# When and by which engine a 65 MB buffer is zeroed in a graph network kernel, and where its node features are loaded

## The reference, cut to what matters

```python
edge_index = jnp.stack([src, dst])
h = jnp.maximum(_layernorm(x, axis=-1), 0.0)
x = x + _L0_gnn_ref(h, src, dst, edge_weight, L0_gnn_kernel, L0_gnn_bias)
# in _L0_gnn_ref:
#   messages = edge_vals[:, None] * transformed[edge_col]
#   aggregated = segment_sum(messages, edge_row, num_segments=N_NODES)   # edge_row = src
```

## Time and profile before

| | us |
|---|---|
| median of 3 runs | 19079.15 (19072.6 to 19079.55) |
| span of the profiled execution | 19095.1 |
| `prepare` until VectorE's first cast | 195.2 |
| `prepare`, rest | 44 |
| `begin` | 60 |
| "gcn_in" | 104 |
| "hist", first block | 221 |

### The profile page before, as it was taken

One profiled execution on the slowest core, in us unless ns is written; L12 is line 12 of the kernel. 1 busy time (PEld: TensorE's weight loads), 2 busy tenths in 40 slices (PEclk: granted clock), 3 DMA queues, 4 the chain that ended last, 5 costly groups with the idle time before them and its releaser, 6 DMA issues. The chain is left out here.

```text
span 19095.1 us, 359029 instructions
## 1 busy us (share of the span) xinstructions
PE 12487.0 (65%) x80127; PEld 9630.4 (50%) x80128; DVE 13169.5 (69%) x30834; ACT 7233.3 (38%) x19056; POOL 11352.9 (59%) x11773
## 2 busy tenths in 40 slices
PE   3543337589998377775777757777587777753333
PEld 2322225456666266664666646666356666433332
DVE  4877778567776688887888878888555555543334
ACT  0111118345555266663666636666331111310000
POOL 0477760067776177773777737777027777047775
PEclk7555555577777555555655555555786666865555
DMA  5233334233334222222222222222672222841112
GB/s 192 62 94 93 94 83 115 61 90 102 103 103 92 52 58 58 58 58 46 58 58 58 58 46 58 58 58 58 240 270 53 53 53 51 337 156 26 26 26 47
DMA packets 1474194, 1652.50 MB, mean 87 GB/s; under 512 B 976447, under 2 KB 1080911, under 8 KB 1442001
## 3 DMA queue, kind: packets, MB, share of 16 engines
q1 hardware_dynamic: 1062709, 1057.28, 18.7%
q0 software_dynamic: 404480, 528.97, 14.0%
q10 hardware_dynamic: 6912, 65.18, 0.8%
HBM read 1028.20 MB, written 626.36 MB: 87 GB/s over the span
## 5 line engine op out<-in xcount | busy, mean ns | idle before, releaser
L1728 POOL DMA_INDIRECT gat_from_src<-gat_src_dram,gat_src_at x4992 | 4825.8, 967 | 2417.3 <-issue 1520.7
L2168 POOL DMA_INDIRECT rel_from_src<-typed_dram,rel_src_at x3328 | 3177.5, 955 | 2386.3 <-ACT rel_src_at L2182 1373.6
L1274 POOL DMA_INDIRECT all_node<-hyp_dst_dram,hyp_src_at x1768 | 1725.7, 976 | 1622.6 <-ACT hyp_src_at L1292 1084.7
L2298 PE MATMUL rel_ps_sum<-all_node,rel_msg 128*64 128x128 f32 x6656 | 1514.3, 403 | 1685.4 <-DVEq L2260 1656.2
L1945 PE MATMUL gat_ps_sum<-all_node,gat_msg 128*80 128x128 f32 x9984 | 2268.0, 420 | 42.1 <-DVE gat_msg L1841 7.5
L2298 PEld LDWEIGHTS rel_ps_sum<-all_node,rel_msg 128*64 128x64 f32 x6656 | 1211.3, 210 | 1936.6 <-DVEq L2260 1513.2
L1945 PEld LDWEIGHTS gat_ps_sum<-all_node,gat_msg 128*80 128x80 f32 x9984 | 2058.3, 251 | 102.3 <-issue 43.3
L776 POOL DMA_INDIRECT bucket_dram<-all_node,order_index x1664 | 1617.6, 972 | 530.8 <-issue 505.9
L1889 DVE TENSOR_TENSOR gat_sums<-gat_sums,gat_ps_sum 80x128 f32 x4992 | 1393.2, 279 | 381.3 <-DVE gat_sums L1889 212.5
L1851 DVE TENSOR_TENSOR_SCAN gat_ps_log<-gat_masks,gat_top,gat_ps_log 8x1024 f32<-8x1024 bf16 x624 | 1462.0, 2343 | 228.3 <-DVE gat_sums L1889 219.6
L1923 PE MATMUL gat_ps_log<-all_ident,gat_leaky 128*8 128x128 f32 x4992 | 1069.9, 387 | 727.0 <-DVE gat_leaky L1836 727.0
(11 more groups left out here) (445 smaller groups left out, 27294.7 us busy)
## 6 DMA issues: line engine op xcount, KB each, us to landing
typed_dram<-typed_res SPq DMA_DIRECT2D x200, 2144.0 KB
gat_relrow<-in_rows_dram SPq DMA_DIRECT2D x624, 256.0 KB
all_node<-gcn_table_dram SPq DMA_DIRECT2D x1664, 48.0 KB
gat_from_src<-gat_src_dram,gat_src_at POOLq DMA_INDIRECT x4992
bucket_dram<-by_dst_zero ACTq DMA_DIRECT2D x48, 1326.0 KB
gsum_rec<-bucket_dram SPq DMA_DIRECT2D x221, 288.0 KB
all_node<-lo_rows_dram SPq DMA_DIRECT2D x221, 256.0 KB
rel_table<-inv_count_dram SPq DMA_DIRECT2D x1664, 32.5 KB
```

Of the source, the lines that this page charges most:

```text
L1274: nc.gpsimd.indirect_dma_start(from_dst[:, q, k, :], None, g.hyp_dst[:, :], bass.IndirectOffsetOnAxis(ap=src_at[:, q, k:k + 1], axis=0)).t ...
L1728: nc.gpsimd.indirect_dma_start(from_src[:, q, k, :], None, g.gat_src[:, :], bass.IndirectOffsetOnAxis(ap=src_at[:, q, k:k + 1], axis=0)).t ...
L2168: nc.gpsimd.indirect_dma_start(from_src[:, q, k, :], None, g.typed[:, :], bass.IndirectOffsetOnAxis(ap=src_at[:, q, k:k + 1], axis=0)).the ...
L2298: last = nc.tensor.matmul(ps_sum[0:D, k, :], msg[:, q % 2, k, :], member[:, q, k, :], start=True, stop=True)
```

## The change

- The 48 clears move from ScalarE to POOL. A new function `clear_buckets` issues a part of them. It has two semaphores in turn, and before a clear it waits until the clear two before it has landed, so that at most two are under way.
- Clears 0 to 7 are issued at the end of POOL's stream of `prepare`, after waits for the seven edge tiles and for the node features. Clears 8 to 17 are issued in `begin`, clears 18 to 47 in the first block of "hist", after the iota.
- The node features are loaded in `prepare`, on SP right behind the seven edge tiles and ahead of SP's wait for the masks, into a buffer `g.x_all` that both phases share. VectorE sets its tail before it sets the tile of zeros. `begin` has no load and no wait for one.
- `rows` is no tile of its own any more but the same memory as `raw`, seen as floats: VectorE's casts run in place.
- In "order" POOL waits for two semaphores instead of one.

```diff
+def clear_buckets(nc, g, pool, first, last):
+    rows = g.bucket.rearrange("(p w) f -> p (w f)", p=P)
+    for n in range(first, last):
+        if n >= 2:
+            pool.wait_ge(g.zeroed[n % 2], 16 * (n // 2))
+        nc.gpsimd.dma_start(rows[:, n * ZERO:(n + 1) * ZERO], g.zero[:, :]).then_inc(g.zeroed[n % 2], 16)
...
 def prepare(nc, g):
-        rows = [ph.sb(f"rows{n}", [P, EB, P]) for n in range(5)]
+        rows = [raw[n][:, :, :].bitcast(F32) for n in range(5)]
...
                 nc.gpsimd.tensor_copy(g.iota16[:, :], g.iota[:, :])
+                pool.wait_ge(padded, 7)
+                pool.wait_ge(rows_in, 7 * 16)
+                pool.wait_ge(x_in, 32)
+                clear_buckets(nc, g, pool, 0, 8)
...
                                  ).then_inc(rows_in, 16)
+                sp.wait_ge(padded, 7)
+                full, rest = N // P, N % P
+                sp.dma_start(g.x_all[:, 0:full, :], g.x[0:full * P, :].rearrange("(t p) d -> p t d", p=P)).then_inc(x_in, 16)
+                sp.dma_start(g.x_all[0:rest, full, :], g.x[full * P:N, :]).then_inc(x_in, 16)
                 sp.wait_ge(stored, 1)
...
-            @block.scalar
-            def _(act):
-
-                act.wait_ge(padded, 6)
-                flat = g.bucket.rearrange("(p w) f -> p (w f)", p=P)
-                for n in range(CLEARS):
-                    act.dma_start(flat[:, n * ZERO:(n + 1) * ZERO], g.zero[:, :]).then_inc(g.zeroed, 16)
...
                 nc.vector.memset(padf[:, :], 0.0).then_inc(padded, 1)
+                nc.vector.memset(g.x_all[:, N // P:NT, :], 0.0).then_inc(padded, 1)
                 nc.vector.memset(g.zero[:, :], 0.0).then_inc(padded, 1)
...
 def begin(nc, g):
-        x, sq, stat = ph.sb("x", [P, NT, D]), ph.sb("sq", [P, NT, D]), ph.sb("stat", [P, 2, NT])
+        x, sq, stat = g.x_all, ph.sb("sq", [P, NT, D]), ph.sb("stat", [P, 2, NT])
         with nc.Block() as block:
+            @block.gpsimd
+            def _(pool):
+                clear_buckets(nc, g, pool, 8, 18)
+
             @block.sync
             def _(sp):
-                sp.wait_ge(cleared, 1)
-                sp.dma_start(x[:, 0:full, :], g.x[0:full * P, :].rearrange("(t p) d -> p t d", p=P)).then_inc(loaded, 16)
-                sp.dma_start(x[0:rest, full, :], g.x[full * P:N, :]).then_inc(loaded, 16)
-                sp.wait_ge(loaded, 32)
                 sp.dma_start(nodes_view(g.xs), x[:, :, :]).then_inc(stored, 16)
                 sp.wait_ge(stored, 16)
 
             @block.vector
             def _(dve):
-                nc.vector.memset(x[:, full:NT, :], 0.0).then_inc(cleared, 1)
-                dve.wait_ge(loaded, 32)
...
 def bucket_places(nc, g):
                                allow_small_or_imprecise_dtypes=True).then_inc(numbered, 1)
+                clear_buckets(nc, g, pool, 18, CLEARS)
...
 def edges_ordered(nc, g):
-                pool.wait_ge(g.zeroed, 16 * CLEARS)
+                for s in range(2):
+                    pool.wait_ge(g.zeroed[s], 16 * (CLEARS // 2))
```

More of the change, by code:

```diff
@@ L199, in floor_by @@
     chain(v.tensor_scalar(out, out, MAGIC, None, ALU.subtract))
+def clear_buckets(nc, g, pool, first, last):
[4 more added lines that the diff above has]
+        nc.gpsimd.dma_start(rows[:, n * ZERO:(n + 1) * ZERO], g.zero[:, :]).then_inc(g.zeroed[n % 2], 16)
 def prepare(nc, g):
     with Phase(nc, "prep") as ph:
-        loaded, padded, const, turned, copied, step, stored, rows_in = ph.sems(
-            "loaded padded const turned copied step stored rows_in")
+        loaded, padded, const, turned, copied, step, stored, rows_in, x_in = ph.sems(
+            "loaded padded const turned copied step stored rows_in x_in")
         padi = ph.sb("padi", [P, 16], I32)
@@ L404, in begin @@
     with Phase(nc, "begin") as ph:
-        loaded, step, cleared, stored, asked, given = ph.sems("loaded step cleared stored asked given")
-        x, sq, stat = ph.sb("x", [P, NT, D]), ph.sb("sq", [P, NT, D]), ph.sb("stat", [P, 2, NT])
-        full, rest = N // P, N % P
+        step, stored, asked, given = ph.sems("step stored asked given")
+        x, sq, stat = g.x_all, ph.sb("sq", [P, NT, D]), ph.sb("stat", [P, 2, NT])
         with nc.Block() as block:
+            @block.gpsimd
+            def _(pool):
+                clear_buckets(nc, g, pool, 8, 18)
             @block.sync
             def _(sp):
-                sp.wait_ge(cleared, 1)
-                sp.dma_start(x[:, 0:full, :], g.x[0:full * P, :].rearrange("(t p) d -> p t d", p=P)).then_inc(loaded, 16)
-                sp.dma_start(x[0:rest, full, :], g.x[full * P:N, :]).then_inc(loaded, 16)
-                sp.wait_ge(loaded, 32)
                 sp.dma_start(nodes_view(g.xs), x[:, :, :]).then_inc(stored, 16)
@@ L2401, in gnn_kernel @@
             g.base = own.sb("base", [1, ET], I32)
-            g.zero, g.zeroed = own.sb("zero", [P, ZERO]), own.sem("zeroed")
-            prepare(nc, g)
-            begin(nc, g)
+            g.zero, g.zeroed = own.sb("zero", [P, ZERO]), own.sems("zeroed0 zeroed1")
+            with Phase(nc, "whole") as whole:
+                g.x_all = whole.sb("x_all", [P, NT, D])
+                prepare(nc, g)
+                begin(nc, g)
             project(nc, g, "gcn_in", [w["L0_gnn_kernel"]], [(g.gcn_table, slice(0, D), slice(0, D))],
```

## The result

| | before | changed |
|---|---|---|
| median (range) of 4 runs, us | 19079.35 (19072.6 to 19079.69) | 18918.34 (18915.8 to 18919.41) |
| ratio, 95% interval | | 0.9916 (0.9902 to 0.993) |
| span of the profiled execution | 19095.1 | 18917.7 |
| VectorE's first cast in `prepare` | 195.2 | 47.6 |
| first reduction in `begin` (L386, now L397) | 258.4 | 100.3 |

The changed kernel is 161.0 us faster, where 148 were forecast. (The two profiled executions differ by more, 177.4 us: the one of the kernel before was 16 us slower than its median, and that difference lies in the later stages, see "The two kernels again".) VectorE's timeline of the changed kernel, beside the earlier trace rows, holds most of it. Columns are start, length, instruction, and in brackets the idle time before it with its releaser.

The account below looks back on a forecast made before the run. The first 195 us were taken as a DMA queue, with late-needed clears among urgent transfers. Terms -144 - 17.3 + 5 + 7 + 1 = -148.3 took the profiled span to 18946.8, hence 18931 us, range 18892 to 18980.

Parts of the forecast that it names:

- Part 1: Start of `prepare`: without clears ahead, edge loads land earlier and VectorE starts at 51 us, not 195.2: -144 us.
- Part 2: `begin`: features loaded early behind the edge loads land far ahead, so the wait for them goes: -17.3 us.
- Parts 3 and 4: Clears 0 to 7 in `prepare` +5 us, 8 to 17 in `begin` +7, first loads of "gcn_in" +1.
- SP waits for the stores, so the phase grows: End of `prepare`: SP's wait for mask stores, landing at 101 us against VectorE's 95.3, lengthens it by 5 us.
- the stores land when all of the clears are through: `prepare`: mask stores take turns with the clears and land last, at 101 us or one landing earlier.
- How engines share: DMA engines: one short row of a load moves for each row of the clears, 0.42 us a row.
- Part 5: First block of "hist": thirty clears, 98 us at 3.25 each, stay hidden under VectorE: 0 us.
- The stores aren't held up: Rival for `prepare` and `begin`: stores finish before VectorE, adding 0 there; -160, 18919 us; chance 0.15.
- Slow clears: Rival: POOL, held at its issues by VectorE, takes 5 to 7 us a clear; 18945 us; chance 0.10.
- Cut rows: Rival: POOL cuts clear rows into 512-byte pieces, 20 us a clear; 19567 us; chance 0.03.
- No earlier start: Rival: something other than clears holds SP, so edge loads start no earlier; 19075 us; chance 0.02.
- The sum: Whole kernel: -144 - 17.3 + 5 + 7 + 1 = -148.3 us, giving 18931 us.

Follow-up runs that it names:

- The two kernels again: Kernel before and changed kernel both rerun unchanged on another chip, for second profiles: changed 18904.78 us, 153.7 us below the kernel before, ratio 0.9919.

## Why the prediction was right, and where it wasn't

**Part 1, the edge loads.** Right: L284 is issued at 23.08 (forecast 26), the first cast is at 47.59 (51), so -147.6 us for -144. The copies end at 19.4 us, near the 0.81 + 16 of the forecast; the pads' rows of 16 bytes all run from 19.2 to 21.2 us, 2 us where 4 to 10 were forecast, once nothing stands between them. That it is the clears which held them is shown by the kernel with the clears first.

**Part 2, x.** Right: -17.3 forecast, 15.6 us by time and 17.2 in the trace by itself. That its load must not share its time with the clears wasn't in the forecast; the kernel with x in `begin` shows it as 25 us.

**Parts 3 and 4, the phase ends.** The sizes were right: +5 and +7 +1 were forecast. From the first cast to the first reduction, less the old wait for x, it is 52.7 against 258.42 - 195.19 - 17.47 = 45.8 us, +7; begin's stretch is 51.9 against 44.6, +7.3. The step that failed is "SP waits for the stores, so the phase grows", and with it "the stores land when all of the clears are through". SP is done 4.8 and 3.6 us before each barrier; the stores land at 94.7 and 146.0 us, ahead of the last clears at 98.6 and 148.8. The last one is POOL, which doesn't leave a block before its own clears have landed. By the stores alone the phases would have grown by 2.7 and 4.2 us over VectorE's end. I had counted what POOL issues and what waits for its semaphores, and not what its stream does at the end of a block. So the size was in part luck. It held because stores and clears share one budget of the engines, 26 + 9 and 32.5 + 16 us, which the forecast had right: both come through near its end, whichever lands last. The kernel without waits, with all clears at once, is the one in which the forecast's order is seen.

**How engines share.** One row for one row, as the earlier trace rows had it, as long as many clears are under way. In the trace of the kernel before, 1152 packets end on SP's queue from 120 to 147 us (1136 rows of 512 bytes and 16 of 4) and 1151 on the clears'. In the kernel without waits all eight clears are issued by 66 us, the count from 75 to 85 us is 431 rows against 431 packets, and the stores land after 35 us, the sum of both. With at most two clears under way the stores get on faster, 2335 rows against 315, which the forecast hadn't seen. By the rule of the Trainium skill ("DMA: Bandwidth & Descriptors", section on queues, rings and completion order) that an engine drains some 9 to 17 descriptors at a turn, the stores' 416 rows would have taken 32 turns of 0.41 us beside their own 9, and landed after 22 us; this is an estimate. The measurement disagrees with it.

**Part 5, "hist".** Right: L635 at 972 ns, 3.4 us a clear against 3.25, nothing exposed, also with 48 clears. The granted clock is 0.50 in the first block of "hist", as before.

**The rivals.** "The stores aren't held up" gave 18919 us, and 18918 was measured; but its reason is refuted, the stores were held up for 45.5 us. Slow clears: from the first issue to the last they are 4.1 and 4.5 us apart in the two phases and 3.4 in "hist", not 5 to 7; the issue took 531 ns at the median, beside a busy VectorE too. Cut rows: the number of packets is the same. No earlier start: refuted.

**The sum.** Terms: -147.6 - 17.5 + 7 + 7.3 = -150.8, which is what the start of "gcn_in" shows (302.99 to 152.19). The forecast of -148.3 was of this start, and missed it by 2.5. The other 10 us of the first measurement lie behind it and did not come again: the second pair has 153.7 us in time and 152.6 at "gcn_in". What made these 10 us in the first measurement stays open.

## What to carry to other kernels

Work that is needed late and fills the DMA engines should not be put ahead of small transfers that everything waits for; where a stage without transfers is at hand (here "hist", 220 us long), put all of it there. Splitting it over two earlier stages cost 14 us. Beside a large transfer that always has rows waiting, price a transfer of short rows by its number of rows times the large one's row, up to the whole of the large one. Pacing the large one lets the short rows through sooner, but the stage still has to hold the sum of both. And a stage whose own transfers are under its compute has room for others only as far as the sum of both stays below the compute.

## What the runs showed of the hardware

- POOL doesn't pass the end of a block before its direct transfers have landed: its drain took 8.40 and 8.82 us, and 28.18 and 35.59 without waits between the clears, and it ended 0.8 to 0.9 us after the last packet of the clears each time. ACT's drain with the same transfers took 0.15 us, with over 7 us to go to the last packet; there SP's waits behind its stores fell from 4.8 and 3.6 us to 0.2.
- The engines moved one row of a queue of short rows for each packet of a queue with many large ones: 431 against 431, 861 against 862, 1152 against 1151. With at most two large transfers under way it was 2335 against 315.
- Taking away POOL's drain brought 2.3 of 8 us, since the stores, which it had hidden, then landed 2.6 us later in each phase; the engines' work was the same.
- Eight clears without waits held POOL for 5 us and the issue of SP's third store for 22.28 us, until 90.9 us; the last of these clears ended at 91.3. So an issue can be held by what other queues have put on the engines.
- A clear of 1.36 MB from POOL took 531 ns to issue, less than the 971 ns of an indirect transfer of 128 short rows.
